# First group of a selective-scan layer: each pair's projection, tap, convolution and weight split taken one slot sooner

## The reference

```python
h = x * rsqrt(mean(x * x) + EPS) * norm_w
proj = einsum('bsd,od->bso', h, in_proj_w)           # gate | hidden, B, C | dt
hBC = silu(causal_conv(hBC, conv_w, conv_b))         # 4 taps along the sequence
dt = softplus(dt + dt_bias); A_cs = cumsum(-exp(A_log) * dt)
M = einsum('bcihn,bcjhn->bcijh', Ch, Bh) * exp(segsum(A))
y = einsum('bcijh,bcjhp->bcihp', M, hid * dt) + ... + Dp * hid
yg = y * silu(gate)
ygr = yg * rsqrt(mean(yg * yg over a group) + EPS)
out = einsum('bsd,od->bso', ygr * gnorm_w, out_proj_w)
```

## Time and profile before

| | |
|---|---|
| median of 3 runs | 793.27 us (790.05 to 795.29) |
| the profiled execution: time / span | 791.84 us / 789.7 us |
| PE busy | 774.6 us, 98% of the span |
| POOL busy | 696.3 us, 88% |
| DVE busy | 636.4 us, 81% |
| ACT busy | 596.5 us, 76% |
| DMA | 94.94 MB, mean 120 GB/s |
| granted clock of PE, mean of the span | 0.995 |

### The profile page before, as it was taken

One profiled execution on the slowest core, in us unless ns is written; L12 is line 12 of the kernel. 1 busy time (PEld: TensorE's weight loads), 2 busy tenths in 40 slices (PEclk: granted clock), 3 DMA queues, 4 the chain that ended last, 5 costly groups with the idle time before them and its releaser, 6 DMA issues.

```text
span 789.7 us, 13488 instructions
## 1 busy us (share of the span) xinstructions
PE 774.6 (98%) x4275; PEld 611.2 (77%) x4275; DVE 636.4 (81%) x753; ACT 596.5 (76%) x1055; POOL 696.3 (88%) x553
## 2 busy tenths in 40 slices
PE   8989899999999999999999999999999999999997
PEld 7767677877887777877787777877787778877765
DVE  6888787888879886889779886888778778798875
ACT  5799677788778877788678877787687877788552
POOL 6689999899889998899889998999899998899551
PEclk9999999999999999999999999999999999999999
DMA  8356243344254433444243324434343333431001
GB/s 327 119 159 209 91 135 101 128 135 133 67 160 133 133 111 115 133 131 127 74 160 127 116 99 131 135 113 129 109 133 116 122 123 100 136 114 66 1 2 54
DMA packets 58028, 94.94 MB, mean 120 GB/s; under 512 B 13168, under 2 KB 46064, under 8 KB 58000
## 3 DMA queue, kind: packets, MB, share of 16 engines
q1 hardware_dynamic: 57712, 94.06, 37.6%
q10 hardware_dynamic: 288, 0.52, 0.2%
HBM read 93.26 MB, written 1.31 MB: 120 GB/s over the span
## 4 chain that ended last, share of the span: by engine, by line
PE 90%; POOL 4%; DVE 3%; ACT 2%; issue 1%; DMA 0%; DVEq 0%; POOLq 0%; ACTq 0%
PE ps_z L1222 25%; PE ps_out L1357 21%; PE ps_h L1222 21%; PE ps_y L1344 11%; PE ps_t L1195 4%; POOL win_lo L305 1%; PE ps_out L1195 1%; PE ps_t L1367 1%; DVE conv L814 1%; DMA acc<-in_x 0%; POOL csx L343 0%; POOL wout_lo L310 0%; POOL win_hi L296 0%; PE ps_h L1330 0%; PE ps_t L1330 0%
## 5 line engine op out<-in xcount | busy, mean ns | idle before, releaser
L305 POOL TENSOR_TENSOR win_lo<-w_raw,win_hi 128x1024 fp32r<-128x1024 f32 x64 | 182.0, 2843 | 9.7 <-DMA csx<-cs_rows 4.7
L604 ACT ACTIVATE decay<-csx,cs_own 128x256 f32<-128x256 f32 (+1 forms) x512 | 184.4, 443 | 0.8
L814 DVE SCALAR_TENSOR_TENSOR conv<-ps_h,par,conv 128x510 f32<-128x510 f32 (+2 forms) x192 | 142.9, 744 | 20.0 <-ACT conv L533 15.4
L604 ACT ACT_TABLE_LOAD x63 | 80.8, 1283 | 90.0 <-PE ps_y L1344 82.0
L899 DVE TENSOR_TENSOR decay<-decay,cbm 128x1536 f32<-128x1536 f32 x64 | 145.5, 2273 | 0.3 <-ACT decay L604 0.3
L343 POOL TENSOR_SCALAR_AFFINE_SELECT csx<-csx 128x512 f32<-128x512 f32 x128 | 109.3, 877 | 2.5 <-DMA csx<-cs_rows 2.5
L958 DVE SCALAR_TENSOR_TENSOR v<-hidT,par,ps_y 128x512 f32<-128x512 f32 x64 | 47.8, 747 | 78.3 <-PE ps_y L1344 78.2
L1357 PE MATMUL ps_out<-wout_hi,y_hi 128*128 128x512 f32 x252 | 100.3, 398 | 0.0
L1344 PE MATMUL ps_y<-decay,hid_dt 128*64 128x256 f32 (+1 forms) x1024 | 97.3, 332 | 2.4 <-DVE decay L899 1.3
L1357 PE MATMUL ps_out<-wout_lo,y_hi 128*128 128x512 f32 x252 | 99.6, 395 | 0.0
L1357 PE MATMUL ps_out<-wout_hi,y_lo 128*128 128x512 f32 x252 | 99.3, 394 | 0.0
(11 more groups left out here) (323 smaller groups left out, 1509.6 us busy)
## 6 DMA issues: line engine op xcount, KB each, us to landing
w_raw<-in_wmain SPq DMA_DIRECT2D x64, 768.0 KB, 5.9
csx<-cs_rows SPq DMA_DIRECT2D x128, 256.0 KB, 3.5
bc_raw<-in_wbc SPq DMA_DIRECT2D x8, 517.0 KB, 5.3
...
par<-in_wpar SPq DMA_DIRECT2D x64, 4.0 KB, 3.6
...
out_x<-acc SPq DMA_DIRECT2D x4, 256.0 KB, 2.6
acc<-in_x ACTq DMA_DIRECT2D x2, 256.0 KB, 3.9
```

The lines of the kernel that those rows point to most:

```text
L305: eng.tensor_tensor(win_lo[:, r2, :], w_raw[:, r4, 0:W_IN], win_hi[:, r2, :].bitcast(f32), ALU.subtract).then_inc(low_win, 1)
L604: done = eng.activation(decay[:, r2, b, h, lo:lo + n], csx[:, r2, b, h, lo:lo + n], ACT.Exp, bias=cs_own[:, r2, t, h:h + 1])
L814: eng.scalar_tensor_tensor(out=out_b[:, :, back:], in0=src_b[:, :, 0:S - back], scalar=w[:, TAPS - 1 - back:TAPS - back], in1=out_b[:, :, ...
```

## The change

In the first group only:

- PE: the slots 3 to 6 project h(k+1) behind the output product, and slot 7 projects none. z(k) then stands at the slot's start. B of the next group is projected at the end of slot 6 as before.
- ACT: the slots 3 to 6 run hidden(k), gates(k), finish_y(k), decays(k), tap(k+1), where the slots 4 to 6 had decays(k), tap(k), finish_y(k), hidden(k), gates(k). Slot 7: the tap of B, hidden, finish_y, SiLU of B, gates, decays.
- DVE: conv_hidden(k+1) stands at the end of the slots 3 to 6, behind lower_y; `constants` goes from slot 0 to the end of slot 3.
- POOL: slot k prepares pair k+2 from slot 2 on, with `select` ahead of the splits; in slot 1 `lower_in` of pair 3 also waits for the first mask (`dve_m`).
- SP: the weights of the pairs 4 to 7 are asked for one slot sooner.

The diff, cut to its core:

```diff
@@ sync @@
-                if not (first and k < 4):
+                if not first:
...
+                if first and 3 <= k < PPG - 1:
+                    eng.dma_start(par[:, k + 1, :], wpar_d[s + 1]).then_inc(w_in[(k + 1) % 4], 16)
+                    eng.wait_ge(low_wout, s - 2)
+                    eng.dma_start(w_raw[:, (k + 1) % 4, :], wmain_d[s + 1]).then_inc(w_in[(k + 1) % 4], 16)
@@ gpsimd @@
                     split_in(3, 1)
+                    eng.wait_ge(dve_m, 1)
                     lower_in(3, 1, 4)
...
+                if first and k < PPG - 1:
+                    eng.wait_ge(act_exp, k)
+                    own_sums(k + 1, 1 - r2)
+                    eng.wait_ge(csx_in[1 - r2], 32 * ((k + 1) // 2 + 1))
+                    select(1 - r2)
+                    if k < PPG - 2:
+                        eng.wait_ge(w_in[(k + 2) % 4], 32 * ((k + 2) // 4 + 1))
+                        eng.wait_ge(pe_gate, k + 1)
+                        split_in((k + 2) % 4, r2)
+                        lower_in((k + 2) % 4, r2, k + 3)
...
+                    sum_squares(k, 0, k, True)
+                    split_out(r4)
+                    lower_out(r4, k + 1)
+                    if k == 4:
...
+                        lower_bc(2)
                     return
@@ scalar @@
-                if first and k == 3:
-                    hidden(3, 3)
-                    gates(3, 3)
-                    finish_y(3, 0, 3, True)
-                    decays(3, 3)
+                if first and k < PPG - 1:
+                    hidden(k, k)
+                    gates(k, k)
+                    finish_y(k, 0, k, True)
+                    if k == PPG - 2:
+                        scale_context(0)
+                    decays(k, k)
+                    tap(k + 1, 0, k + 1)
+                    return
+                if first:
+                    tap_bc(0, 1, ps_z, conv_bc[:])
+                    hidden(k, k)
+                    finish_y(k, 0, k, True)
+                    silu_bc(0, 1, conv_bc[:])
+                    gates(k, k)
+                    decays(k, k)
                     return
@@ vector @@
-                    constants()
...
-                if first and k == 3:
-                    combine(3, 3)
-                    scale_hidden(3, 3)
-                    mask(3, 0, 3)
-                    lower_y(3, 3)
+                if first and k < PPG - 1:
+                    combine(k, k)
+                    scale_hidden(k, k)
+                    mask(k, 0, k)
+                    lower_y(k, k)
+                    conv_hidden(k + 1, k + 1)
+                    if k == 3:
+                        constants()
+                    if k == PPG - 2:
+                        quantise_context(0)
                     return
...
-                conv_hidden(s, k)
+                if not first:
+                    conv_hidden(s, k)
@@ tensor @@
-                if first and k < 4:
+                if first and k < PPG - 1:
                     first_pairs(k)
                     return
...
-                if k < 3:
-                    eng.wait_ge(low_win, k + 2)
-                    eng.wait_ge(dve_conv, 3 * k + 3)
-                    project(ps_h[:], win_hi[:, 1 - r2, 0:KT * P], win_lo[:, 1 - r2, 0:KT * P], pe_hid)
-                else:
-                    project_out(3, 0, 3)
+                if k >= 3:
+                    project_out(k, 0, k)
+                eng.wait_ge(low_win, k + 2)
+                eng.wait_ge(dve_conv, 3 * k + 3)
+                project(ps_h[:], win_hi[:, 1 - r2, 0:KT * P], win_lo[:, 1 - r2, 0:KT * P], pe_hid)
...
+                if k == PPG - 2:
+                    project_group(k, 0, k)
@@ project_out @@
+                if isinstance(s, int):
+                    eng.wait_ge(low_wout, s - 2)
```

45 lines of the change are left out of this document (21 added, 24 removed).

## The result

The changed kernel takes 802.39 us in the median of 4 runs (801.17 to 803.86). The ratio to the kernel before is 1.0144, with a 95% interval of 1.0115 to 1.0173: slower by 1.4%. (The kernel before has four runs by now, with a median of 791.9; the 793.27 of the table ahead was that of the first three.) The profiled execution took 802.73 us, span 800.7; that of before 791.84 and 789.7. So the two profiles are 11.0 us apart.

A forecast was written before the change was run, and what follows sets the result against it. PE, busy 98%, bounds the kernel now; the change adds a slower ACT-DVE ring. +7.5 us at z(8) and +1.1 for the clock make +8.6: 800.4 on the profiled 791.84, 801.9 on the median; forecast 801.0, range 794.5 to 804.5.

The forecast's parts named there:

- The ring: ACT and DVE, first group: tap, convolution, `v`, table load, SiLUs, exponentials in series, 11.6 us a slot against PE's 10.3.
- The walk to z(7): First group, slot by slot: `v` and mask times lead to z(7) starting at 110.0, 7.2 us later than before.
- the steps on the context: Slots 6 to 7: context's scale on ACT, 0.81 us, and two DVE steps, 1.54 us, added before `v` of slot 7.
- PE's single waits: PE, first group: 2.2 us at the fourth scan, 1.3 at each of the next two, 9.6 ahead of z(7).
- the clock: PE at z(7): lower granted clock after the long wait costs between nothing and 1.7 us; 1.1 taken.
- The port at slot 7: DVE and POOL share a port: `win_lo` of pair 8 delays `yg` by nothing to 1.9 us; 1.1 taken.
- From z(7) to z(8): ACT's gates, table load, exponentials, tap, and C's convolution put z(8) at 123.4, 7.5 us later than before.
- From there on nothing more is lost: Behind z(8), POOL and ACT have the loop's slack, so no further loss.
- What the profile was to show: Signs: mask waits 1 to 2.5 us, 8 to 11 before z(7), ACT idle until `v`, taps 11.6 apart, no `win_lo` wait.
- The change does what it says: Rival, chance 0.10: PE stays the bound and all first-group waits go, 6.7 us less, 785.1 us.
- The ring binds more cheaply: Rival, chance 0.15: table load starts before the wait for `v` or is hidden, no port taken; ring 10.3 us, time 795.4.
- more is lost: Rival, chance 0.10: `yg` and mask blocked in slot 7 (1.9 + 1.6 us), clock costs 1.7 twice; 805 us.

The follow-up runs named there:

- e1: Changed kernel with the next pair's tap ahead of table load and exponentials on ACT, slots 3 to 6: 795.86 us, ratio 1.0047.
- e2: Changed kernel with `v` of the next pair ahead of that pair's convolution on DVE, slots 3 to 6: 798.45 us, ratio 1.0082.
- e11: Changed kernel with `constants` back in slot 0 of DVE, ahead of the first mask: 801.14 us, ratio 1.0127.
- e4: Changed kernel with two more POOL waits: `win_lo` of pairs 6 and 8 wait for the masks of slots 4 and 7: 800.86 us, ratio 1.0114.
- e9: Changed kernel, six moves: tap early; B's convolution behind `v`; B/C split in slot 5, ahead of output split; `win_lo` of pair 8 behind mask; constants in slot 5: 787.78 us.
- e10: Changed kernel with 146 thrown-away matmuls on PE ahead of z(7): 800.31 us, ratio 1.0115.
- e7: Kernel before, with POOL's split of the B and C weights at the end of slot 5 instead of 4, first group: 792.93 us, ratio 1.0014.
- e12: e9 plus a seventh move: in slot 7 ACT takes its exponentials directly behind the tap of B: 787.71 us, ratio 0.9944.

## Why the prediction was right

**The ring: right.** Worked out as 11.6 us a slot, it measures 11.47 (taps at 74.25 and 85.72). It was named as the whole mechanism, and e1 and e2, which cut it at two places, give back 7.7 and 4.9 us.

**The walk to z(7): right within 0.6 us, partly since errors cancel.** z(7) was put at 110.0 and came at 109.47. The starts of `v` can be set side by side: foreseen 65.45, 77.05, 88.65 and 102.55 in the slots 4 to 7, measured 65.81, 77.27, 88.74 and 101.71. At slot 4 the constants were longer than taken and the tap 0.5 us earlier; at slot 7 the steps on the context were shorter; behind it the port cost more than taken. PE's single waits were wrong: the fourth scan waited 3.93 us instead of 2.2, the fifth and sixth not at all instead of 1.3 each, and z(7) 6.32 us instead of 9.6, since PE itself came to it 2.8 us later than foreseen (103.15 instead of 100.4). DVE and POOL at the fourth scan:

```profile
64.03 1.20 DVE L951 CAST onesr<-onesf 1x128 fp32r<-1x128 f32 x1
...
68.55 3.31 DVE L930 TENSOR_TENSOR decay<-decay,cbm 128x1536 f32<-128x1536 f32 x1
```

```profile
67.57 2.67 POOL L310 TENSOR_TENSOR win_lo<-w_raw,win_hi 128x1024 fp32r<-128x1024 f32 x1
```

The constants took 2.8 us (63.02 to 65.81), not the 1.8 taken: the cast to `onesr`, 0.21 us in the kernel before, took 1.20. And the mask of slot 4 was blocked by `win_lo`, for 1.6 us, a term that the walk had for slot 7 only. This made PE late enough, the clock's fall behind it included, that the later masks were in time. PE's waits ahead of z(7) do not add to the loss, since z(7) goes by the ring on ACT and DVE and not by PE; what delays `v` does (e11).

**The port at slot 7: the right size, another instruction.**

```profile
102.59 0.69 DVE L998 TENSOR_TENSOR yg<-v,gate 128x512 f32<-128x512 f32 x1
...
103.80 3.31 DVE L930 TENSOR_TENSOR decay<-decay,cbm 128x1536 f32<-128x1536 f32 x1
```

`yg` came 0.5 us ahead of `win_lo` (103.13 to 105.49) and was not held, `hid_dt` at 103.19 took its usual 0.68 us beside it, and the mask behind them was held, by 1.6 us where 1.1 were taken. The two steps on the context took 0.42 and 0.43 us, where the rows of before have 0.85 and 0.74; from the first of them to `v` it is 0.79 us instead of 1.54. The prediction had cited the rule of the Trainium skill (SBUF — State Buffer, Who interferes with whom) that the first to issue has the pair of ports for its whole length; both halves of it are in these rows. By that rule the 1.1 us would have turned to nothing; the trace agrees for `yg` and shows a later instruction, the mask, paying instead. e4, which keeps `win_lo` off this mask, has 1.55 us less between `v` and z(7).

**From z(7) to z(8): the step that was too short.** The prediction put 13.4 us there, and 1.1 for the clock beside it; the profile has 17.54. Two terms are missing in "gates 0.6, table load 1.3, exponentials of the pairs 7 and 8 5.65, tap of C 0.8, convolution 2.3". One is the second table load, 1.28 us, at the loop's entry; with it and some tenths between instructions it is 15.1 us, and 15.1 is what e1, e9 and e10 show with the clock up. The other is the clock: 1.1 was taken, between nothing and 1.7, because the one wait to be seen had cost 1.7. It cost 2.4 (17.5 less 15.1; e10). The bound was wrong, since a wait of 6.3 us need not be followed by as short a stretch of the low level as one of 2.68.

**"From there on nothing more is lost": right**, to 0.9 us over fourteen profiles (last column of the table).

**The sum.** Forecast at z(8) were +7.5 + 1.1 = 8.6 us, measured are 11.1 (127.01 less 115.89), 2.5 more: 1.7 for the path behind z(7) (15.1 less 13.4) and 1.3 for the clock (2.4 less 1.1), less 0.5 for z(7). In the medians it is 802.39 against the 801.0 forecast. That these lie within 1.4 us is in part luck: the loss was put 2.5 us too low, and the base that it was added to, the 793.27 of three runs, was 1.4 us above the 791.9 of four.

**What the profile was to show.** Three of its signs failed by their numbers: the waits for the mask in the slots 4 to 6, "1 to 2.5 us each", are 3.93 us once and then none; the wait ahead of z(7), "8 to 11 us", is 6.32; and a wait for `win_lo`, which was to be a sign of being wrong, is there with 0.39 and 0.53 us. The idle time ahead of `hidden`'s table load, ended by `v`, and the distance of the taps held, the latter only between the pairs 5 and 6 (11.47): the turn with the constants took 14.24 us and the one with the context 12.18.

**The rivals.** "The change does what it says" falls: the waits of 2.68 us for `win_lo` and of 1.27 and 1.09 us ahead of the scans went, and the time rose. "The ring binds more cheaply" falls with 11.47. Of "more is lost" the clock's part came true, the port's in half. What e7 adds: without the ring, taking away the longest of the three waits by itself gains nothing; that more was to be had, with the right moves together, e9 and e12 show. The drain of about 1380 ns that the Trainium skill (ScalarE: Activation LUTs, What ACT_TABLE_LOAD costs) adds to each load does not show here: the load at 115.58 ends at 116.86, and the exponentials start at 116.87.
